# A gated delta-rule attention between two slot FFNs: the turns of the query in transpose mode, fill instructions in the first turn, and a new order of all groups

## The chip, the cores and the metric

The kernel runs on one core of a Trainium2 chip. The metric is the device time of one execution in microseconds; the time of the kernel before is the median of 3 runs. Everything is float32.

## What is computed

```python
x = L0_attn_x                                   # (2, 4096, 512)
x = x + 0.5 * ffn(layernorm(x))                 # slot FFN: route each token to 8 of 64 slots, pool, GRU, read back
x = x + attn(layernorm(x))                      # below
x = x + 0.5 * ffn(layernorm(x))
# attn, 16 heads of 32, for every token t:
#   q, k l2-normalised;  a = sigmoid(x Wa + ba);  b = sigmoid(x Wb + bb)
#   state = a * state + k (b * (v - state^T k))^T ;  y = state^T q
#   out = (rmsnorm(y, g_norm) * silu(x Wg)) @ Wo
```

The slots of an FFN depend on all tokens, so the program has three passes over the tokens: the routing of the first FFN, then one loop that does the first FFN's output, the attention and the routing of the second FFN, then the second FFN's output.

## The kernel before

The sequence is cut into 32 blocks of 128 tokens (`NT`), each for 2 batches (`b`). The middle loop has one turn for each block; in a turn stand pieces of up to four blocks, which the code calls `p` (the newest: FFN output, layer norm, projections of k, q, v), `q` (decays, gram matrices of keys and queries, and the inverse of the 32x32 coupling of each chunk), `r` (the attention itself and its output) and `s` (routing of the second FFN). A block's attention is done in 4 chunks of 32 tokens (`NC`), with 32x32 tiles of TensorE for each head.

Every engine has its order written out by hand: `step_pe`, `step_act`, `step_dve`, `step_pool` and `step_sp` list the calls of one turn, `first_...` and `last_...` those of the ends. An engine does its list strictly in order, and semaphores join the lists: `S[name]` counts what has been done for all blocks and batches, and `free(...)` in a function of TensorE waits until the PSUM bank that it writes has been read by its last user. The bank of each result is in the tables `..._at` (8 banks of 128x512).

The calls that matter here, with the line by which the profile names them:

- `proj_k`, `proj_q`, `proj_va`, `proj_vb` (L847) and `proj_g` (L891): the projections, full 128x128 weights; `first_xT`, `last_xT` (L690): turns of the normalised input, by `nc.tensor.transpose`.
- `gram` (L926), `apply_uw` (L945), `apply_gy` (L976, L983), `chain` (L996): 32x32 tiles. `apply_uw` needs the inverse, which comes through DRAM (`inverse_out`, `inverse_in`, L537).
- `qe_T` (L961): a matmul of the decayed query (`qa`) with the identity, which puts the turned query under the sums of `apply_gy`; two for a part, two parts for each batch.
- `cum` (L899, L901) and `dec` (L911): running sums of the decays; `out_proj` (L1011), `y_norm` (L1004); `hidden` (L1028), `logits` (L1040), `slots` (L1048), `alpha_T` (L1051): the second FFN's routing; `ffn` (L836): the first FFN's output.
- On ScalarE `gate_of` (L1667), `last_gelu` (L1726), `query_square` (L1648), `dec_exp` (L1684). On VectorE `last_top` (L2327 on), `last_weights` (L2336 on), `second_sum` (L2570), `invert` (L2540, L2542), `reading` (L2527), `chunk_kept` (L2553), `state` (L2559), `first_sum` (L2441), `query_turn` (L2508). On GpSimd `query_power` (L1977).

Of the kernel before, what the change touches and what calls it, by code (L numbers as in the profile page):

```python
# [27 lines left out]
P = 128  # L28
# [7 lines left out]
def build(nc, x, Wq, Wk, Wv, Wa, ba, Wb, bb, Wg, Wo, g_norm, slot_init, slot_scale, w1, b1, w2, b2,  # L36
          wih, whh, bih, bhh, wv, bv, wo, bo, tau, out):
    ctx = ExitStack()
    with ctx:
# [169 lines left out]
        ffn_at = [banks(1, 1), banks(2, 1)]  # L209
        xT_at = [banks(1, 1), banks(7, 1)]  # L210
        k_at = [banks(6, 1), banks(0, 1)]
        q_at = [banks(4, 1), banks(4, 1)]
        va_at = [banks(1, 1), banks(5, 1)]
        vb_at = [banks(5, 1), banks(4, 1)]
        g_at = [banks(0, 1), banks(7, 1)]
        dec_at = [banks(5, 1), banks(0, 1)]
        ones_at = [banks(1, 1)[:, 0:1], banks(6, 1)[:, 0:1]]
        wo_at = [banks(2, 1), banks(0, 1)]
        rxT_at = [banks(1, 1), banks(0, 1)]
        h_at = [banks(3, 1), banks(2, 1)]  # L220
        lg_at = [banks(7, 1)[:, 0:NS], banks(0, 1)[:, 0:NS]]
        y_at = [banks(6, 2), banks(5, 2)]
        cum_at = banks(6, 1)[:, 0:8 * H]
        aT_at = banks(4, 1)[:, 0:P]
        slot_at = banks(2, 1)
        gram_at = [[banks(1, 1), banks(5, 1)], [banks(4, 1), banks(3, 1)]]
        uw_at = [[banks(0, 1), banks(7, 1)], [banks(1, 1), banks(5, 1)]]
        gq_at = [[banks(3, 1), banks(2, 1)], [banks(0, 1), banks(1, 1)]]
# [172 lines left out]
        def _(sp):  # L401
# [188 lines left out]
            def last_sp():  # L590
                store_second(NT - 2, 0)
                hold(NT - 1, 0)
                store_second(NT - 2, 1)
                store_alpha(NT - 3)
# [3 lines left out]
                inverse_in(NT - 1, 1)  # L598
                coupling_out(NT, 0)
# [5 lines left out]
                store_alpha(NT - 2)  # L605
# [3 lines left out]
                inverse_in(NT, 1)  # L609
                drain_loads()  # L610
# [5 lines left out]
            def first_sp():  # L616
# [4 lines left out]
                load_first(2, 0)  # L621
                load_first(2, 1)
                coupling_out(1, 0)
                coupling_out(1, 1)
                coupling_in(1)
                hold(1, 0)
                load_alpha(3)
                load_first(3, 0)
                hold(1, 1)
                inverse_out(1)  # L630
                load_first(3, 1)
# [5 lines left out]
                store_second(1, 0)  # L637
                hold(2, 0)
                load_alpha(4)
                store_second(1, 1)  # L640
                load_first(4, 0)
                hold(2, 1)
                inverse_out(2)
                load_first(4, 1)
# [25 lines left out]
            for t in range(4, NT):  # L670
                step_sp(t + 1, t, t - 1, t - 2, t - 3)
# [13 lines left out]
        def _(pe):  # L685
# [2251 lines left out]
```

## Time and profile before

| | |
|---|---|
| time, median of 3 runs | 2709.87 us (2707.37 to 2710.03) |
| profiled execution | 2713.64 us, its span 2711.0 us |
| TensorE busy | 2597.6 us, 96% of the span |
| VectorE, GpSimd, ScalarE busy | 68%, 49%, 41% |
| granted TensorE clock, mean | 0.985 |

The span has a routing pass of some 300 us, the middle loop from 310.5 us to about 2640 us, and the last pass. Matmuls are pipelined: a row's duration reaches to the modelled end of the last one, so the pace of TensorE is read from the start of one row to the start of the next. In a timeline a row merges neighbours of one line: start, length, engine, line, operation, names, shape, and in brackets how long the engine was idle before it and who ended that. A float32 matmul stands in the trace as two passes, each with its own weight load; a transpose as one.

### The profile page before, as it was taken

How to read it: one execution, taken by the hardware profiler on the slowest of the kernel's cores; microseconds unless marked ns; L12 is line 12 of the kernel's file. 1: busy time of each engine (PE TensorE's matmuls, PEld its weight loads, DVE VectorE, ACT ScalarE, POOL GpSimd, SP SyncE). 2: the span in 40 equal slices, each digit the busy share in tenths (PEclk: the TensorE clock that was granted, in tenths of full speed). 3: DMA queues.
4: the chain of work that ended last, by engine and by line, in shares of the span. 5: the costliest groups of instructions: out<-in, count | busy, mean ns of one | idle time of the engine just before them, and what ended most of it. 6: DMA issues, size and time to landing. Idle time of an engine off the chain costs nothing.

```text
span 2711.0 us, 116416 instructions
## 1 busy us (share of the span) xinstructions
PE 2597.6 (96%) x51052; PEld 1857.1 (69%) x51052; DVE 1849.7 (68%) x5306; ACT 1122.9 (41%) x2024; POOL 1334.0 (49%) x1767
## 2 busy tenths in 40 slices
PE   7999879999999999999999999999999999999868
PEld 5788557777766677677766676777667777776643
DVE  6778456776777766676666666666666776777626
ACT  5777324343333333444334444443444334333320
POOL 2222255555555555555555555555555555555510
PEclk9999989999999999999999999999999999999979
DMA  7443022222222222222222222222222222222178
GB/s 232 113 133 115 22 57 66 67 67 67 67 67 61 60 61 63 58 67 67 67 67 67 65 64 66 55 60 62 64 67 67 67 67 67 67 67 58 52 265 326
DMA packets 365963, 224.74 MB, mean 83 GB/s; under 512 B 277584, under 2 KB 294032, under 8 KB 365456
## 3 DMA queue, kind: packets, MB, share of 16 engines
q1 hardware_dynamic: 356240, 200.51, 26.6%
q10 hardware_dynamic: 9216, 16.78, 1.6%
q8 instruction: 402, 6.59, 1.0%
q14 instruction: 105, 0.86, 0.1%
HBM read 125.49 MB, written 74.97 MB: 74 GB/s over the span
## 4 chain that ended last, share of the span: by engine, by line
PE 62%; DVE 15%; issue 10%; ACT 6%; POOL 5%; SPq 1%; DMA 1%; DVEq 0%; ACTq 0%; POOLq 0%
PE psum L847 14%; PE psum L945 5%; PE psum L1011 4%; PE psum L926 4%; PE psum L891 4%; PE psum L976 4%; PE psum L996 4%; PE psum L983 3%; DVE blk L2542 3%; DVE blk L2540 3%; PE psum L753 2%; PE psum L911 2%; PE psum L961 2%; PE psum L1028 2%; POOL sm L1977 2%
## 5 line engine op out<-in xcount | busy, mean ns | idle before, releaser
L847 PE MATMUL psum<-w_all,xnT 128*128 128x512 f32 (+2 forms) x2048 | 751.0, 501 | 6.7 <-DVE pk L2527 6.0
L1977 POOL TENSOR_TENSOR sm<-sm,half 128x1 f32<-128x1 f32 (+1 forms) x384 | 537.0, 1398 | 142.6 <-ACT sm L1672 126.6
L847 PEld LDWEIGHTS psum<-w_all,xnT 128*128 128x128 f32 x2048 | 366.4, 191 | 229.4 <-issue 178.6
L2540 DVE TENSOR_TENSOR blk<-blk 128x30 f32<-128x30 f32 (+14 forms) x960 | 328.0, 342 | 37.1 <-issue 10.6
L2542 DVE TENSOR_TENSOR blk<-blk 128x30 f32<-128x30 f32 (+14 forms) x960 | 324.0, 338 | 33.0
L2009 POOL TENSOR_SCALAR sm<-sm 128x1 f32<-128x1 f32 x64 | 22.4, 351 | 541.1 <-DVE sm L2447 541.1
L891 PEld LDWEIGHTS psum<-xnT,w_all 128*128 128x128 f32 x2048 | 246.7, 191 | 49.1 <-issue 39.9
L891 PE MATMUL psum<-xnT,w_all 128*128 128x128 f32 x2048 | 273.7, 282 | 0.0
L1011 PE MATMUL psum<-w_out,gate 128*128 128x512 f32 x512 | 260.7, 612 | 0.0
L996 PEld LDWEIGHTS psum<-qg,st 32*32 32x32 f32 x8192 | 127.4, 105 | 94.9 <-issue 55.5
L2492 DVE TENSOR_REDUCE sm<-scr 128x16 f32<-128x512 f32 x64 | 43.9, 686 | 201.4 <-ACT scr L1648 201.4
L1695 ACT ACTIVATE qg<-psum 128x256 f32<-128x256 f32 x128 | 42.1, 381 | 322.7 <-PE psum L976 322.7
L996 PE MATMUL psum<-qg,st 32*32 32x64 f32 x8192 | 167.9, 218 | 6.3 <-issue 3.8
L926 PE MATMUL psum<-kqT 32*32 32x64 f32 x8192 | 148.0, 215 | 5.5 <-DVE kqT L2508 2.1
L976 PE MATMUL psum<-pk,uw 32*32 32x64 f32 x8192 | 144.4, 224 | 7.4 <-issue 6.4
L983 PE MATMUL psum<-pk,uw 32*32 32x64 f32 x8192 | 149.6, 225 | 0.7 <-issue 0.7
L926 PEld LDWEIGHTS psum<-kqT 32*32 32x32 f32 x8192 | 124.2, 105 | 38.1 <-issue 26.7
L1028 PEld LDWEIGHTS psum<-rxT,w1T 128*128 128x128 f32 x1024 | 131.1, 194 | 19.9 <-issue 15.3
L945 PEld LDWEIGHTS psum<-vk,E 32*32 32x32 f32 x8192 | 120.8, 105 | 29.1 <-issue 25.2
L1028 PE MATMUL psum<-rxT,w1T 128*128 128x128 f32 x1024 | 140.1, 281 | 0.0
L976 PEld LDWEIGHTS psum<-pk,uw 32*32 32x32 f32 x8192 | 99.9, 103 | 54.4 <-issue 32.8
L945 PE MATMUL psum<-vk,E 32*32 32x64 f32 x8192 | 134.8, 215 | 0.0
(278 smaller groups left out, 4726.4 us busy)
## 6 DMA issues: line engine op xcount, KB each, us to landing
blk<-n_scratch SPq DMA_DIRECT2D x64, 512.0 KB, 4.2
xin<-in_L_attn_x_dram SPq DMA_DIRECT2D x96, 256.0 KB, 3.0
n_scratch<-nn SPq DMA_DIRECT2D x64, 256.0 KB, 4.1
xh<-xc SPq DMA_DIRECT2D x64, 256.0 KB, 2.2
e_scratch<-blk SPq DMA_DIRECT2D x32, 512.0 KB, 2.9
E<-e_scratch SPq DMA_DIRECT2D x64, 256.0 KB, 3.9
x_scratch<-xh SPq DMA_DIRECT2D x62, 256.0 KB, 2.5
rxn<-in_L_attn_x_dram SPq DMA_DIRECT2D x32, 256.0 KB, 3.0
```

Source lines behind the costliest of these rows:

```text
L847: last = mm(dst, xnT[b][:, k * P:(k + 1) * P], w_all[:, k * WK + at:k * WK + at + n], start=(k == 0), stop=(k == KC - 1))
L891: last = mm(g_at[b][:, part * P:(part + 1) * P], w_all[:, at:at + P], xnT[b][:, k * P:(k + 1) * P], start=(k == 0), stop=(k == KC - 1))
L926: last = mm(q32(gram_at[b][part], c, at, 2 * HD), q32(kqT[b], c, h * 2 * HD, HD), q32(kqT[b], c, h * 2 * HD, 2 * HD), start=True, stop=True)
L945: last = mm(q32(uw_at[b][part], c, at, 2 * HD), q32(E[b], c, h * HD, HD), vk3[b][CH * c:CH * (c + 1), n % 2::2 - n % 2, h, :], start=True, ...
L976: last = mm(q32(gq_at[b][hb // 2], hq, (hb % 2 * NC + c) * 2 * HD, 2 * HD), q32(uw[b], c, at + HD, HD), q32(pk[b], c, at, 2 * HD), start=F ...
L983: last = mm(q32(y_at[b], hq, (hb * NC + c) * 2 * HD, 2 * HD), q32(uw[b], c, at, HD), q32(pk[b], c, at, 2 * HD), start=(hb % 2 == 0 and r = ...
L996: last = mm(q32(y_at[b], hq, at, 2 * HD), q32(st[b], hq, x * P + hb * HD, HD), q32(qg[b], hq, at, 2 * HD), start=False, stop=True, skip_gr ...
L1011: last = mm(wo_at[b], gate[b][:, part * P:(part + 1) * P], w_out[:, part * D:(part + 1) * D], start=(part == 0), stop=(part == KC - 1))
L1028: last = mm(h_at[b][:, part * P:(part + 1) * P], w1T[:, k * HID + part * P:k * HID + (part + 1) * P], rxT[b][:, k * P:(k + 1) * P], start= ...
L1977: return g.tensor_tensor(dst, a, half[:, 0:n], ALU.pow)
L2540: own(tt(o, Y[:, 0:rows, s_:s_ + 1].to_broadcast([P, rows, cols]), N[:, s_:s_ + 1, s_ + 1:CH].to_broadcast([P, rows, cols]), ALU.mult))
L2542: ins = tt(Y[:, 0:rows, s_ + 1:CH], Y[:, 0:rows, s_ + 1:CH], o, ALU.add)
```

## The change

What it does:

- `qe_T` gets `is_transpose=True`, and waits on its own semaphore for its query.
- `fill(56, 1)`: 56 small matmuls and one turn of the identity into a free bank, between `ffn(1)` and `first_xT(1, 0)`.
- All PSUM places are dealt out anew, and with them the users that `free(...)` waits for.
- The orders of all five engines are written anew. On TensorE `cum(q)` goes ahead of `dec(q, 1)`, `logits(s, 1)` behind the first half of `out_proj(r, 0)`, `apply_gy(r, 0, 0)` beside `apply_gy(r, 0, 1)`, and `proj_vb(q, 1)`, `proj_g(q, 1, 2)`, `ffn(p)`, `alpha_T(s)` to other places. On ScalarE `gate_of(q, 1)` goes ahead of `last_gelu(r, 0)`. On the SP queue `load_first` and `load_alpha` come later.
- The loop's turn is cut elsewhere (`range(5, NT + 1)`), so more stands in `first_...`. The calls are the same ones, as often, but for `fill`.

```diff
-        g_at = [banks(0, 1), banks(7, 1)]
+        g_at = [banks(4, 1), banks(3, 1)]
-        lg_at = [banks(7, 1)[:, 0:NS], banks(0, 1)[:, 0:NS]]
+        lg_at = [banks(3, 1)[:, 0:NS], banks(7, 1)[:, 0:NS]]
-        y_at = [banks(6, 2), banks(5, 2)]
+        y_at = [banks(6, 2), banks(6, 2)]
-        gram_at = [[banks(1, 1), banks(5, 1)], [banks(4, 1), banks(3, 1)]]
+        gram_at = [[banks(0, 1), banks(3, 1)], [banks(4, 1), banks(1, 1)]]
...
             def proj_g(n, b, part):
                 if part == 0:
+                    pe.wait_ge(S["xnT"], both(n, b))
                     if b == 0:
-                        free((n - 1, (T["qg"][1], nth(n - 1, 0))), (n, (S["draw"], both(n, 1))))
+                        free((n, (T["pt"][1], nth(n, 0))))
+                    else:
+                        free((n - 1, (S["yv"], both(n - 1, 0))), (n, (T["pt"][0], nth(n, 1))))
...
             def qe_T(n, b, part):
+                pe.wait_ge(S["qe"], both(n, b))
...
                     mm(eight(gq_at[b][part])[:, k * NC:(k + 1) * NC, 0:HD], qa[b][:, hb * P:(hb + 1) * P],
-                       ident[:, :].rearrange("p (c e) -> p c e", c=NC), start=(k == 0), stop=False, skip_group_check=True)
+                       ident[:, :].rearrange("p (c e) -> p c e", c=NC), start=(k == 0), stop=False, is_transpose=True,
+                       skip_group_check=True)
...
             def logits(n, b):
                 pe.wait_ge(S["hT"], both(n + NT, b))
                 if b == 0:
-                    free((n + 1, (S["gate"], both(n + 1, 1))), (n, (S["ysq"], both(n, 0))))
+                    free((n + 1, (S["gate"], both(n + 1, 1))), (n, (S["yv"], both(n, 0))))
                 else:
-                    free((n + 2, (S["draw"], both(n + 2, 1))), (n + 1, (T["uw"][0], nth(n + 1, 0))), (n, (S["rxnT"], both(n + NT, 1))))
+                    free((n + 1, (S["ysq"], both(n + 1, 0))), (n, (S["ysq"], both(n, 1))))
...
+            def fill(n, turned):
+                for i in range(n):
+                    c = i % NC
+                    mm(q32(y_at[1], c, i // NC % 8 * 2 * HD, HD), q32(ident, c, c * HD, HD), q32(ident, c, 0, HD), start=True, stop=True)
+                for c in range(turned):
+                    tr(q32(y_at[1], c, 0, HD), q32(ident, c, c * HD, HD), q32(ident, c, c * HD, HD))
...
             def first_pe():
                 ffn(1)
+                fill(56, 1)
                 first_xT(1, 0)
...
                 chain(r, 0, 1)
                 gram(q, 0, 2)
                 chain(r, 0, 2)
+                gram(q, 0, 3)
+                cum(q)
                 dec(q, 1)
-                gram(q, 0, 3)
-                logits(s, 1)
                 chain(r, 0, 3)
...
                 apply_uw(r, 1, 0)
-                cum(q)
                 out_proj(r, 0, 0)
+                out_proj(r, 0, 1)
+                logits(s, 1)
                 apply_uw(r, 1, 1)
...
+                proj_g(q, 1, 0)
+                proj_g(q, 1, 1)
                 slots(s)
-                proj_g(q, 1, 0)
                 apply_gy(r, 1, 2)
                 apply_gy(r, 1, 3)
-                proj_g(q, 1, 1)
+                proj_vb(q, 1, 0)
+                proj_g(q, 1, 2)
                 proj_g(q, 0, 0)
-                ffn(p)
                 chain(r, 1, 0)
```

The order of TensorE from the chains of `r`, batch 0 (L996 before, L1013 after), over the grams of `q` (L926, L938) to the output projection (L1011, L1032), before:

```order
L996 MATMUL psum<-qg,st 32x64 x16
L911 MATMUL psum<-dr,after 128x512
L926 MATMUL psum<-kqT 32x64 x16
L1040 MATMUL psum<-w2T,hT 128x64 x2
L996 MATMUL psum<-qg,st 32x64 x16
L926 MATMUL psum<-kqT 32x64 x64
L945 MATMUL psum<-vk,E 32x64 x16
L899 MATMUL psum<-gt,before 128x32
L899 MATMUL psum<-gt,upto 128x32
L899 MATMUL psum<-gt,after 128x32
L901 MATMUL psum<-glx,ones 32x32 x4
L1011 MATMUL psum<-w_out,gate 128x512
```

and of the change:

```order
L1013 MATMUL psum<-qg,st 32x64 x16
L938 MATMUL psum<-kqT 32x64 x16
L909 MATMUL psum<-gt,before 128x32
L909 MATMUL psum<-gt,upto 128x32
L909 MATMUL psum<-gt,after 128x32
L911 MATMUL psum<-glx,ones 32x32 x4
L921 MATMUL psum<-dr,after 128x512
L1013 MATMUL psum<-qg,st 32x64 x16
L938 MATMUL psum<-kqT 32x64 x64
L959 MATMUL psum<-vk,E 32x64 x16
L1032 MATMUL psum<-w_out,gate 128x512 x2
L1065 MATMUL psum<-w2T,hT 128x64 x2
```

The running sums (L899, L901) move from behind the grams to ahead of them, and the logits of `s` (L1040, L1065) from ahead of them to behind them.

The order of TensorE in the second half of the turn, from the last pieces of `apply_gy` of `r`, batch 1, to the first chains, before:

```order
L976 MATMUL psum<-pk,uw 32x64 x16
L983 MATMUL psum<-pk,uw 32x64 x16
L891 MATMUL psum<-xnT,w_all 128x128 x8
L836 MATMUL psum<-sv,aT_in 128x512 x2
L996 MATMUL psum<-qg,st 32x64 x16
L891 MATMUL psum<-xnT,w_all 128x128 x8
```

and of the change:

```order
L993 MATMUL psum<-pk,uw 32x64 x16
L1000 MATMUL psum<-pk,uw 32x64 x16
L848 MATMUL psum<-w_all,xnT 128x256 x2
L902 MATMUL psum<-xnT,w_all 128x128 x8
L1013 MATMUL psum<-qg,st 32x64 x16
L902 MATMUL psum<-xnT,w_all 128x128 x4
```

The gate projection of batch 0 (the second four of the first L891 row; the second four of L902) now stands behind half of `proj_vb` and ahead of the same chain; `ffn` (L836) has left this place.

The order of ScalarE near the turn's end, before:

```order
L1672 ACTIVATE sm<-psum,eps 128x1
L1715 ACTIVATE rxn<-xh,sm 128x512
L1726 ACT_TABLE_LOAD
L1726 ACTIVATE hT<-psum,h_bias 128x128 x2
L1667 ACT_TABLE_LOAD
L1667 ACTIVATE gate<-psum 128x512
L1720 ACTIVATE rxT<-psum 128x512
```

and of the change:

```order
L1707 ACTIVATE sm<-psum,eps 128x1
L1702 ACTIVATE gate<-psum 128x512
L1761 ACT_TABLE_LOAD
L1761 ACTIVATE hT<-psum,h_bias 128x128 x2
L1750 ACTIVATE rxn<-xh,sm 128x512
L1773 ACTIVATE aT_out<-psum 128x128
L1755 ACTIVATE rxT<-psum 128x512
```

The gate of `q`, batch 1 (L1667, L1702) goes ahead of the gelu (L1726, L1761), and one table load is gone there.

## Rows read from the trace of the kernel before

**Rows 1.** The page: the span.

```profile
span 2711.0 us, 116416 instructions
```

**Rows 2.** Windows, the loop's 28 turns: busy of PE, PEld, DVE, ACT, POOL, then the clock.

```profile
461.05:2437.67 1976.62, 1962.16 (x42757) 1390.18 (x42756) 1380.71 (x3781) 798.17 (x1401) 1106.48 (x1401) 1.00 0.25 64
```

**Rows 3.** Timeline of PE at the end of one turn.

```profile
1158.39 1.02 PE L847 MATMUL psum<-w_all,xnT 128*128 128x512 f32 x2
1159.64 0.63 PE L1040 MATMUL psum<-w2T,hT 128*128 128x64 f32 x4 [0.22 <-ACT gate L1667]
1160.10 1.08 PE L847 MATMUL psum<-w_all,xnT 128*128 128x256 f32 x4
1161.02 0.61 PE L961 MATMUL psum<-ident,qa 128*128 128x128 f32 x4
1161.47 1.06 PE L1028 MATMUL psum<-rxT,w1T 128*128 128x128 f32 x8
1162.36 1.02 PE L847 MATMUL psum<-w_all,xnT 128*128 128x512 f32 x2
1163.22 1.05 PE L1028 MATMUL psum<-rxT,w1T 128*128 128x128 f32 x8
1164.11 0.60 PE L690 MATMUL psum<-ident,xn 128*128 128x128 f32 x4
1164.55 1.14 PE L847 MATMUL psum<-w_all,xnT 128*128 128x288 f32 x4
...
1166.06 1.15 PE L945 MATMUL psum<-vk,E 32*32 32x64 f32 x68
```

**Rows 4.** Timelines from the last query projection to the grams of batch 1.

```profile
1110.24 0.65 PE L996 MATMUL psum<-qg,st 32*32 32x64 f32 x32
...
1112.08 2.92 POOL L1977 TENSOR_TENSOR sm<-sm,half 128x16 f32<-128x16 f32 x1
...
1115.83 0.71 DVE L2508 STREAM_TRANSPOSE kqT<-qs 128x512 f32<-128x512 f32 x1
...
1116.69 1.99 PE L926 MATMUL psum<-kqT 32*32 32x64 f32 x128
```

**Rows 5.** Timeline of PE behind those grams.

```profile
1118.47 0.65 PE L945 MATMUL psum<-vk,E 32*32 32x64 f32 x32
1119.05 0.41 PE L899 MATMUL psum<-gt,before 128*128 128x32 f32 x2
...
1120.04 1.12 PE L1011 MATMUL psum<-w_out,gate 128*128 128x512 f32 x2
...
1131.92 2.05 PE L891 MATMUL psum<-xnT,w_all 128*128 128x128 f32 x16
```

**Rows 6.** Timeline of DVE in the same stretch.

```profile
1119.08 0.27 DVE L2327 SCALAR_TENSOR_TENSOR lgt<-psum,itau,b2s 128x64 f32<-128x64 f32 x1
...
1122.77 0.98 DVE L2336 TENSOR_TENSOR lgt<-lgt 128x64 f32<-128x64 f32 x1 [0.35 <-ACT lgt L1733]
...
1126.81 0.75 DVE L2570 SCALAR_TENSOR_TENSOR xh<-psum,sm,xh 128x512 f32<-128x512 f32 x1 [1.59 <-POOL sm L1977]
...
1132.19 0.75 DVE L2553 TENSOR_TENSOR qg<-psum,qa 128x256 f32<-128x256 f32 x2 [0.32 <-ACT qg L1695]
1132.86 0.41 DVE L2527 TENSOR_TENSOR pk<-psum,dm 128x256 f32<-128x256 f32 x1
```

**Rows 7.** The inverse's load: L537's landing times, and its issue in this turn.

```profile
DMA to landing us min/median/max: 3.1/3.9/4.8
...
1161.54 1.98 SPq L537 DMA_DIRECT2D E<-e_scratch  x2
```

**Rows 8.** The first turn: timeline of PE, and a window (PE, PEld, DVE, ACT, POOL, clock).

```profile
315.72 1.12 PE L690 MATMUL psum<-ident,xn 128*128 128x128 f32 x4 [4.09 <-ACT xn L1623]
317.53 12.05 PE L847 MATMUL psum<-w_all,xnT 128*128 128x512 f32 x28 [0.69 <-ACT xnT L1628]
...
315.30:322.00 6.70, 5.59 (x10) 2.90 (x11) 0.00 (x0) 0.97 (x2) 0.91 (x3) 0.50 0.09 32
```

More of the change, by code:

```diff
@@ L1181, in last_pe @@
                 apply_uw(NT - 1, 1, 0)
-                cum(NT)
                 out_proj(NT - 1, 0, 0)
+                out_proj(NT - 1, 0, 1)
+                logits(NT - 2, 1)
                 apply_uw(NT - 1, 1, 1)
@@ new lines, in first_pe @@
+                gram(3, 1, 3)
+                apply_uw(2, 1, 0)
+                out_proj(2, 0, 0)
+                out_proj(2, 0, 1)
+                logits(1, 1)
+                apply_uw(2, 1, 1)
+                apply_uw(2, 1, 2)
+                apply_uw(2, 1, 3)
+                qe_T(2, 1, 0)
+                out_proj(2, 0, 2)
+                out_proj(2, 0, 3)
+                y_norm(2, 0)
+                qe_T(2, 1, 1)
+                apply_gy(2, 1, 0)
+                apply_gy(2, 1, 1)
@@ new lines, in first_pe @@
+                proj_g(3, 1, 0)
+                proj_g(3, 1, 1)
+                slots(1)
+                apply_gy(2, 1, 2)
+                apply_gy(2, 1, 3)
+                proj_vb(3, 1, 0)
+                proj_g(3, 1, 2)
+                proj_g(3, 0, 0)
+                chain(2, 1, 0)
+                proj_g(3, 0, 1)
+                last_xT(2, 0)
+                chain(2, 1, 1)
+                proj_g(3, 0, 2)
+                ffn(4)
+                chain(2, 1, 2)
+                proj_vb(3, 1, 1)
@@ new lines, in first_pe @@
+                proj_g(3, 0, 3)
+                chain(2, 1, 3)
+                proj_g(3, 1, 3)
+                hidden(2, 0, 0)
+                out_proj(2, 1, 0)
+                out_proj(2, 1, 1)
+                first_xT(4, 0)
+                out_proj(2, 1, 2)
+                y_norm(2, 1)
+                proj_k(4, 0, 0)
+                out_proj(2, 1, 3)
+                proj_k(4, 0, 1)
+                proj_k(4, 0, 2)
+                alpha_T(1)
+                hidden(2, 0, 1)
+                proj_q(4, 0, 0)
@@ new lines, in first_pe @@
+                proj_k(4, 0, 3)
+                logits(2, 0)
+                proj_q(4, 0, 1)
+                proj_vb(4, 0, 0)
+                proj_q(4, 0, 2)
+                proj_vb(4, 0, 1)
+                last_xT(2, 1)
+                proj_q(4, 0, 3)
+                proj_va(4, 0, 0)
+                hidden(2, 1, 0)
+                hidden(2, 1, 1)
+                qe_T(3, 0, 0)
+                first_xT(4, 1)
+                proj_va(4, 0, 1)
+                proj_va(4, 1, 0)
+                apply_uw(3, 0, 0)
```

1004 lines of the change are left out of this document (480 added, 524 removed).

## The prediction

> **What bounds the kernel now.** I read the windows first. Over 28 turns of the middle loop [rows 2] TensorE is busy 1962.16 of 1976.62 us at a granted clock of 1.00, while VectorE has 1380.71, GpSimd 1106.48 and ScalarE 798.17. The window is that of the loop's own 28 turns (`range(4, NT)`), so a turn takes 1976.62 / 28 = 70.6 us, and TensorE sets it. Busy is not pace, though: what counts is how far one row's start lies behind the start of the row ahead. So the timeline came next. There the rows hold hidden waits as well as work: two passes of 512 columns take 1163.22 - 1162.36 = 0.86 us, but from 1158.39 to the logits at 1159.64 it is 1.25 us, and the row names ScalarE's gate as what was waited for [rows 3]. The last view is what the other engines do between two such points.
>
> It shows that a turn has two kinds of stretch. From the end of the last query projection to the grams of batch 1 it takes 1116.69 - 1110.24 = 6.45 us [rows 4], and that is no work of TensorE: ScalarE's square and VectorE's sums of the query come first, then the power on GpSimd, which takes 2.92 us and ends at 1115.00, and VectorE's turn of the query ends at 1116.54, 0.15 us ahead of the grams. Whatever TensorE does meanwhile, this latency stays. The other 70.6 - 6.45 = 64.1 us are TensorE's, and only what leaves those counts.
>
> **The change, part by part, for a turn.**
>
> Turns of the query. `qe_T` is four calls in a turn, each of two matmuls, four passes, in 1161.47 - 1161.02 = 0.45 us. The nearest operation in transpose mode, `first_xT`, does four whole 128-column turns in 1164.55 - 1164.11 = 0.44 us, one pass each [rows 3]. So a call goes from 0.45 to 0.22 us; four calls give 4 x 0.225 = 0.90 us, all in the 64.1 us. The bounds are 0 (the output is written in four pieces of 32 columns, which no row in this mode has) and 0.90; I take 0.90, since pass count is what the rows differ in. The Trainium skill, "TensorE: Matmul & The Clock Gate", in its table of terms calls transpose mode four times faster for FP32; the rows show a factor of two. By the page the gain would be about 1.35 us a turn.
>
> Running sums and logits. `cum` takes 1120.04 - 1119.05 = 0.99 us [rows 5], and it moves from the 64.1 us into the 6.45 us, where there is room: TensorE's own rows there come to about 5.9 us. The output projection behind it stands alone between tile groups, and its row is 1.12 us long where the same two passes among their like make 1.02 [rows 3, 5]; two of them stand together now, so 0.1 us goes with it. `logits(s, 1)` goes the other way: 1160.10 - 1159.64 = 0.46 us [rows 3], with the border to a tile group, 0.1, 0.56 us. Net -0.99 - 0.10 + 0.56 = -0.53 us. The one excursion from tiles to full weights that the new order saves (13 instead of 14) falls in the 6.45 us and is worth nothing.
>
> The wait for the gate. `logits(r, 0)` waited 1.25 - 0.86 = 0.39 us, because the gate of `q` stood behind the gelu and a table load on ScalarE. In the new order it stands ahead, so the wait goes: -0.39 us.
>
> What is new. `last_top(s, 1)` on VectorE started at 1119.08, 0.61 us behind the end of the grams at 1118.47 [rows 5, 6]. Its logits now come only after one tile group (1119.05 - 1118.47 = 0.58), two output projections (1.82 with borders) and themselves (0.56): 2.96 us, some 0.2 more until read, so at +3.15 us. VectorE's list stands behind it: routing weights, `second_sum(r, 0)`, the inverse, `chunk_kept`, `reading(q, 1, 0)`, the states. From 1119.08 to the end of the weights at 1126.81 - 1.59 = 1125.22 it was 6.14 us, of which 0.35 were a wait for an exponential, and that may now come in time. So `second_sum` starts at +3.15 + 5.8 to 6.1 = +9.0 to +9.3 instead of +8.34, because the 1.59 us of waiting ahead of it [rows 6] absorbs most. That moves `reading(q, 1, 0)`, which ended at 1132.86 + 0.41 = +14.8 us, to about +15.3 (0.7 to 0.95 later, less the wait of 0.32 us ahead of `chunk_kept` [rows 6], which absorbs some as well). And `proj_g(q, 0, 0)` now writes the bank that `reading(q, 1, 0)` reads. It began one call behind 1131.92, at +14.1 to +14.4 us; now it loses 0.99 of `cum`, 0.45 of two turns of the query and some 0.3 of borders, and gets 0.56, 0.86 (`proj_vb`) and 0.89 (`proj_g`) ahead of it: +14.7. It waits about 0.6 us. Behind it on TensorE stand the chains of batch 1, `ffn(p)` and `first_xT(p, 0)`. `first_sum(p, 0)` moved behind `invert(q, 13, 16)`, 2.5 us later, and the normalised input would be ready about +27.2 to +28.3; TensorE comes there at about +28.1 once it has waited the 0.6, so I charge the two once. Bounds: 0 (VectorE in time) and 2.5 us (its whole delay of 3.15 - 0.61); I take +0.6.
>
> The inverse. `apply_uw(q, 0, 0)` started at 1166.06, 4.52 us behind the issue of its load at 1161.54, which lands after 3.1 to 4.8 us, the batch-0 half first [rows 3, 7]. So it has about 1 us to spare. TensorE gets there 1.2 us sooner; VectorE's waits that TensorE caused (for the chains and for the second output projection) shrink by about as much. I take 0, bounds 0 and +0.6.
>
> Other moves: `proj_vb`, `alpha_T`, `load_first` and `load_alpha` (still 3 us and more ahead of their users), 0 each, and small waits, ±0.1.
>
> Sum for a turn: -0.90 - 0.53 - 0.39 + 0.60 = -1.2 us (-1.22).
>
> Number of turns. 28 are in the window; the first and the last ones, where TensorE waits more, count for about 2 more: 30 x 1.22 = 36.6 us.
>
> The first turn. TensorE was idle 4.09 us ahead of `first_xT(1, 0)` [rows 8]; the fill (112 short passes) fits in there. The granted clock was 0.50, the 1.2 GHz level, from 315.3 to 322.0 us, and projections started at 317.53, so 4.5 us went at half pace: keeping the clock would be worth 2.2 us, bounds 0 and 2.8. In turn two, `first_sum(2, 0)` comes 2.5 us later, which work moved ahead of it repays in part. I take -1 for both together. The ends: 0, ±4.
>
> Total -37.6 us. The profiled execution took 2713.6 us (its span 2711.0 [rows 1] and 2.6 around it), 3.8 over the median of the runs. 2713.6 - 37.6 = 2676.0, and on the scale of the median 2672.3. I say 2673.
>
> **Rivals.** About 0.2% (5.4 us) is what a measurement can tell from no change.
>
> 1. The forecast, -0.8 to -1.5 us a turn, 2664 to 2686: chance 0.50.
> 2. VectorE is in time after all (the ops of `last_weights` were slowed by GpSimd's work beside them, and it is spread otherwise now), so the 0.6 doesn't appear: -1.8 us a turn, 54 us with 30 turns, 2655. For it: the delay is a difference of sums of some 15 us each. Down to 2640 if the 6.45 us shrink too. 0.22.
> 3. The inverse binds: `apply_uw` waits for its load, and a turn can only lose the spare 1 us less what VectorE loses by the later `last_top`, 0.3 to 0.7 us: -9 to -21 us, 2689 to 2701. For it: the slack is small in each turn. Against it: VectorE's list waited for TensorE in that stretch. 0.12.
> 4. The transposes cost what the matmuls did: -0.3 us a turn, 2700. Against it: no row has such a matmul in one pass at two passes' pace. 0.05.
> 5. Slower: the late logits. If `proj_g(q, 0, 0)` and the chains behind it take VectorE's whole 2.5 us, a turn gets 2.5 - 1.82 = 0.7 us longer, 21 us in all, 2731. It decides once the wait there is over 1.8 us. Against it: the 1.59 us of waiting ahead of `second_sum`, which must stay necessary for some other reason, such as the output projection or GpSimd's power coming later. 0.07.
> 6. The clock. 17 turns by TensorE stand in each turn of the loop already, 8 more come, and the granted clock is 1.00 throughout [rows 2]. Should a stretch of 6.7 us at the lower level, as in [rows 8], come once a turn, it would cost up to 3.3 us a turn, 100 us: 2810. The Trainium skill, on the same page under "PE-mode transpose", says that this mode doesn't count as busy for the clock; by that rule this would be its way. 0.01. What is left, 0.03, is no change within 5.4 us by small waits that eat it up.
>
> The range: 8 in 10 takes rivals 1 and 2 and the nearer part of 3: 2646 to 2697. Faster by over 0.2%: 0.50 + 0.22 + 0.12 + 0.05, less what 3 and 4 have near 2704, so 0.88. Slower 0.08, the same 0.04.
>
> **What would show it.** The window of 28 turns at 69.4 us each. L976 (the new `qe_T`) 256 passes in all instead of 512, two of them in 0.22 us. No wait for the gate ahead of `logits(r, 0)`. A wait of about 0.6 us for `reading` ahead of `proj_g(q, 0, 0)`, VectorE idle some 2.4 us ahead of `last_top(s, 1)` and none ahead of `second_sum(r, 0)`. 6.4 to 6.5 us from the last query projection to the grams. The clock at 1.00 from 315 to 322 us. Wrong would be: `apply_uw` waiting for the inverse, the 6.45 us changed, or a wait of more than 1 us at a place not named.

## Result: 0.7% slower

The changed kernel takes 2730.09 us (median of 7 runs, 2722.05 to 2735.78) against 2710.03 us (median of 7, 2707.37 to 2717.83) on the same chip: ratio 1.0066, 95% interval 1.0046 to 1.0085. I had forecast 2673 us. The order did what was worked out at nearly every place, and yet a turn, measured between the same points of turns 2 and 32, went from 70.5 us to 71.2 us instead of 69.4.

The page of the changed kernel, its span, its busy times and one queue of section 3 (packets, MB, share), beside [rows 1]:

```profile
span 2731.6 us, 116548 instructions
PE 2560.2 (94%) x50909; PEld 1828.3 (67%) x50909; DVE 1841.9 (67%) x5306; ACT 1053.9 (39%) x1962; POOL 1328.8 (49%) x1767
q8 instruction: 402, 6.59, 1.0%
```

TensorE's groups by line, kernel before. The columns are busy us, mean ns, then the idle time ahead of them and what ended it; L976 and L983 are the two halves of `apply_gy`, L926 is `gram`, L945 `apply_uw`:

```profile
L983 PE MATMUL psum<-pk,uw 32*32 32x64 f32 x8192 | 149.6, 225 | 0.7 <-issue 0.7
L926 PE MATMUL psum<-kqT 32*32 32x64 f32 x8192 | 148.0, 215 | 5.5 <-DVE kqT L2508 2.1 <-ACT dr L1684 2.1
L976 PE MATMUL psum<-pk,uw 32*32 32x64 f32 x8192 | 144.4, 224 | 7.4 <-issue 6.4 <-ACT uw L1689 0.7
L945 PE MATMUL psum<-vk,E 32*32 32x64 f32 x8192 | 134.8, 215 | 0.0
```

The same view of the changed kernel (L993 and L1000 `apply_gy`, L938 `gram`, L959 `apply_uw`), with `proj_g` (L902) and the query's turns (L976):

```profile
L902 PE MATMUL psum<-xnT,w_all 128*128 128x128 f32 x2048 | 279.8, 284 | 24.7 <-DVE pk L2562 24.7
...
L938 PE MATMUL psum<-kqT 32*32 32x64 f32 x8192 | 158.9, 216 | 11.0 <-issue 7.7 <-DVE kqT L2543 1.3 <-DVE kn L2523 1.1
L1000 PE MATMUL psum<-pk,uw 32*32 32x64 f32 x8192 | 152.2, 225 | 30.1 <-issue 30.1
L993 PE MATMUL psum<-pk,uw 32*32 32x64 f32 x8192 | 150.6, 224 | 17.3 <-issue 16.5 <-ACT uw L1724 0.4
L959 PE MATMUL psum<-vk,E 32*32 32x64 f32 x8192 | 140.1, 217 | 18.5 <-issue 14.4 <-DMA E<-e_scratch 4.2
...
L976 PE MATMUL psum<-ident,qa 128*128 128x128 f32 x256 | 53.8, 292 | 0.0
```

The reader is to see the word "issue". It is idle time that no wait for an engine or a transfer explains. In these four small-tile lines it was 0.7 + 6.4 = 7.1 us in all, and is 7.7 + 30.1 + 16.5 + 14.4 = 68.7 us. The difference, 61.6 us, is about what separates forecast and result (57 us).

Where does it stand? Timeline of TensorE in the changed kernel, the two `apply_gy` that now stand side by side, first in one turn, then in the turn before it:

```profile
1179.03 0.45 PE L993 MATMUL psum<-pk,uw 32*32 32x64 f32 x32
1179.29 0.54 PE L1000 MATMUL psum<-pk,uw 32*32 32x64 f32 x29
...
1180.01 0.26 PE L1000 MATMUL psum<-pk,uw 32*32 32x64 f32 x4
1181.33 0.43 PE L1000 MATMUL psum<-pk,uw 32*32 32x64 f32 x25 [1.06 <-issue]
1181.68 0.70 PE L848 MATMUL psum<-w_all,xnT 128*128 128x512 f32 x1
```

```profile
1109.44 0.45 PE L993 MATMUL psum<-pk,uw 32*32 32x64 f32 x32
1109.70 0.54 PE L1000 MATMUL psum<-pk,uw 32*32 32x64 f32 x29
...
1110.42 0.49 PE L1000 MATMUL psum<-pk,uw 32*32 32x64 f32 x29
1110.84 1.98 PE L848 MATMUL psum<-w_all,xnT 128*128 128x512 f32 x4
```

The last L1000 row breaks in two behind its fourth pass: 1.06 us idle in the middle of a group of equal passes, of one call, with no wait in the code there. In the other turn it runs through. No semaphore stands there that could do it.

**The theory.** TensorE's instructions come in packets through queue q8, and TensorE idles where the next packet is late. I numbered all of TensorE's records (weight loads, passes, semaphore instructions) in order of time. There are 103084; divided by 256 that is 402.7, and q8 moved 402 packets, of 16384 bytes each in the trace, 64 bytes an instruction. The gaps of changing length, in both kernels, stand at records whose number leaves 192 on division by 256, to within two records. Such a place is called a border here, and the 256 records between two borders a group. There are 402 borders in either kernel, 403 in `fill120` and 400 in `b_transp` (two of the runs below), each time as many as q8 has packets; why the rest is 192 and not 0 no run tells. Of TensorE's idle stretches over 0.15 us between 320 and 2640 us, those at a border add up to 10.9 us in the kernel before and to 72.1 us in the changed one. The Trainium skill, "Advanced Engine Details and Errata", section "ISA Cache", gives an instruction cache line as 16 KB or 256 instructions; the trace agrees with that size. In both kernels a turn has exactly 3072 = 12 x 256 records, so the twelve borders stand at the same instructions in every turn. The times of q8's packets show the rest: a packet starts about 0.9 us after the border ahead of it when nothing disturbs it, takes 0.9 to 1.4 us, and no group starts sooner than about 1.2 us after its packet's end, in either kernel. So a group whose next packet starts behind its border needs about 3.2 us (an estimate from these three); full-width work takes 5 to 20 us for one, but 128 passes of 32x32 tiles, with their weight loads, take 3 to 4, and if the packet is late TensorE runs dry. With the n-th packet taken with the n-th border, in the loop of the kernel before no packet of 337 starts more than 2 us behind its border, and 82 start ahead of it; in the changed kernel 83 of 335 start more than 2 us behind.

The same records, by place in the turn: gap at the border, in ns, from the start of one pass to the start of the next, mean of 23 turns and from the least to the most, and how long behind the border the next packet starts, in us. In brackets stand the block (a dot for any), the batch and the piece.

```
changed kernel        gap (ns)           next packet     before           gap (ns)
ahead of apply_uw      112               +2.33           ffn(p)           446 (318-534)
apply_uw(q,0)          402 (35-1501)     +2.38           gram(q,1)         34
apply_gy(q,0,1)        889 (11-1545)     +2.83           gram(r+1,0)       60
gram / apply_gy(q,0,3) 367 (16-1121)     +1.43           apply_uw(1)       35
gram(.,0,3)            226 (67-630)      +1.54           apply_gy          11
gram(.,1)              101 (24-195)      +1.22           apply_gy          27
apply_gy(.,1,1)         11               +2.52           apply_gy(.,1,2)  168 (8-528)
apply_gy(.,1,2)        654 (73-1156)     +1.87           others           as without a border
```

Less what such a place takes anyway (11 to 36 ns, and 109 ahead of `apply_uw`), that is 2.49 us a turn in the changed kernel. In the kernel before it is 0.16 in `apply_gy` and 0.41 in `ffn`, which took 1.47 us on average there and takes 1.06 in every turn of the changed kernel, where no border stands in it: 0.57. The difference, 1.92 us a turn, times 30 is 57.6 us.

Four packets start 2.3 us and more behind their border. Two of them have large transfers beside them: the one ahead of `apply_uw(q,0,0)` has the two loads of E (the inverse that `apply_uw` needs, L537 before), and the one at `apply_gy(.,1,1)` the loads of the coupling that `invert` works on. The other two, in `apply_uw(q,0)` and `apply_gy(q,0,1)`, have no transfer beside them and stand right behind the first. DMA view of the changed kernel from 1030.9 to 1036.18 us (busy tenths in 40 slices):

```profile
DMA  0599999999998999999999961000001000000000
```

The border is at 1031.7, the engines are full until 1033.9, the packet starts at 1033.76, and `apply_gy(q,0,1)` then has a gap of 1.27 us. The two go together in 26 of 27 turns: in the four in which this packet starts by +0.76 us, `apply_gy(q,0,1)` has no gap, and in the 22 in which it starts at +2.04 us or later, the gap is 0.99 to 1.55 us.

### The profile page after: what moved, and what is told of

It is laid out like the page before. It is cut to its first block, busy times and chain, and to the rows that moved or that the text cites. A ratio compares the mean times of both kernels' runs of the same rounds, so it can differ in the third digit from the quotient of the medians.

```text
span 2731.6 us, 116548 instructions
## 1 busy us (share of the span) xinstructions
PE 2560.2 (94%) x50909; PEld 1828.3 (67%) x50909; DVE 1841.9 (67%) x5306; ACT 1053.9 (39%) x1962; POOL 1328.8 (49%) x1767
## 4 chain that ended last, share of the span: by engine, by line
PE 77%; DVE 9%; issue 6%; POOL 4%; ACT 1%; DMA 1%; SPq 1%; POOLq 0%; DVEq 0%; ACTq 0%
PE psum L848 25%; PE psum L902 7%; PE psum L1032 6%; PE psum L1013 5%; PE psum L1053 4%; PE psum L938 4%; PE psum L959 4%; PE psum L690 3%; PE psum L1000 3%; PE psum L993 3%; PE psum L753 2%; PE psum L921 2%; DVE blk L2577 2%; DVE blk L2575 2%; PE psum L835 1%
## 5 line engine op out<-in xcount | busy, mean ns | idle before, releaser
L2575 DVE TENSOR_TENSOR blk<-blk 128x30 f32<-128x30 f32 (+14 forms) x960 | 332.4, 346 | 61.0 <-issue 34.5
L2577 DVE TENSOR_TENSOR blk<-blk 128x30 f32<-128x30 f32 (+14 forms) x960 | 334.7, 349 | 33.0
L902 PE MATMUL psum<-xnT,w_all 128*128 128x128 f32 x2048 | 279.8, 284 | 24.7 <-DVE pk L2562 24.7
L902 PEld LDWEIGHTS psum<-xnT,w_all 128*128 128x128 f32 x2048 | 253.0, 193 | 42.7 <-issue 27.7
L2044 POOL TENSOR_SCALAR sm<-sm 128x1 f32<-128x1 f32 x64 | 14.9, 233 | 495.1 <-DVE sm L2482 495.1
L1032 PE MATMUL psum<-w_out,gate 128*128 128x512 f32 x512 | 250.6, 603 | 0.0
L1013 PEld LDWEIGHTS psum<-qg,st 32*32 32x32 f32 x8192 | 126.3, 105 | 117.3 <-issue 61.3
L1000 PE MATMUL psum<-pk,uw 32*32 32x64 f32 x8192 | 152.2, 225 | 30.1 <-issue 30.1
L1013 PE MATMUL psum<-qg,st 32*32 32x64 f32 x8192 | 168.0, 218 | 6.7 <-issue 2.6
L938 PE MATMUL psum<-kqT 32*32 32x64 f32 x8192 | 158.9, 216 | 11.0 <-issue 7.7
L993 PE MATMUL psum<-pk,uw 32*32 32x64 f32 x8192 | 150.6, 224 | 17.3 <-issue 16.5
L1724 ACT ACTIVATE uw<-psum 128x512 f32<-128x512 f32 x128 | 76.5, 597 | 220.8 <-PE psum L959 220.8
L938 PEld LDWEIGHTS psum<-kqT 32*32 32x32 f32 x8192 | 130.4, 105 | 46.1 <-issue 38.4
L959 PE MATMUL psum<-vk,E 32*32 32x64 f32 x8192 | 140.1, 217 | 18.5 <-issue 14.4
L993 PEld LDWEIGHTS psum<-pk,uw 32*32 32x32 f32 x8192 | 104.8, 103 | 76.3 <-issue 75.5
L959 PEld LDWEIGHTS psum<-vk,E 32*32 32x32 f32 x8192 | 123.9, 106 | 34.6 <-issue 27.7
L1053 PE MATMUL psum<-rxT,w1T 128*128 128x128 f32 x1024 | 133.9, 280 | 2.4 <-ACT rxT L1755 1.6
L1000 PEld LDWEIGHTS psum<-pk,uw 32*32 32x32 f32 x8192 | 112.2, 103 | 33.7 <-issue 33.7
```

The lines of the kernel that those rows point to most:

```text
L902: last = mm(g_at[b][:, part * P:(part + 1) * P], w_all[:, at:at + P], xnT[b][:, k * P:(k + 1) * P], start=(k == 0), stop=(k == KC - 1))
L938: last = mm(q32(gram_at[b][part], c, at, 2 * HD), q32(kqT[b], c, h * 2 * HD, HD), q32(kqT[b], c, h * 2 * HD, 2 * HD), start=True, stop=True)
L959: last = mm(q32(uw_at[b][part], c, at, 2 * HD), q32(E[b], c, h * HD, HD), vk3[b][CH * c:CH * (c + 1), n % 2::2 - n % 2, h, :], start=True, ...
L993: last = mm(q32(gq_at[b][hb // 2], hq, (hb % 2 * NC + c) * 2 * HD, 2 * HD), q32(uw[b], c, at + HD, HD), q32(pk[b], c, at, 2 * HD), start=F ...
L1000: last = mm(q32(y_at[b], hq, (hb * NC + c) * 2 * HD, 2 * HD), q32(uw[b], c, at, HD), q32(pk[b], c, at, 2 * HD), start=(hb % 2 == 0 and r = ...
L1013: last = mm(q32(y_at[b], hq, at, 2 * HD), q32(st[b], hq, x * P + hb * HD, HD), q32(qg[b], hq, at, 2 * HD), start=False, stop=True, skip_gr ...
```

## Experiments

Eleven kernels ran. The rivals were the semaphore waits (the late logits and `proj_g`'s wait for VectorE, rival 5 of the prediction), the fill instructions themselves, and the two `apply_gy` side by side. The clock is looked at with `before_128`.

**Moving the borders and nothing else.** A fill matmul has four records, so 64 more move every border by a whole packet, and 32 fewer by half of one.

```diff
-                fill(56, 1)
+                fill(120, 1)        # fill120;  fill24: fill(24, 1)
```

> The changed kernel with 120 fill instructions in the first turn in place of 56. Every later instruction of TensorE's stream moves on by 256 records (64 more fill instructions of 4 records each), one whole 16384-byte packet of the instruction queue, so the borders between packets stand at the same instructions as in the changed kernel. Border theory (TensorE waits where one packet's 256 instructions are run through faster than the next packet comes): a turn stays 71.1 us, the time 2728 to 2734 us with at most 3 us for the longer fill. Rival (waits for semaphores, set by VectorE and late logits, make the loss): the same. A control for the next run: if this one moves by more than 5 us, the fill itself matters and not the borders.

> The changed kernel with 24 fill instructions in place of 56: nothing else differs, but every packet border of TensorE's instruction stream stands 128 instructions later in the turn. Border theory: the waits in the middle of L1000, L993 and L959 vanish from their places and others stand 128 instructions away; worked out from the gaps of one turn, two packets of the 12 would then last only 1.4 to 1.8 us, so I expect the time to move by more than 10 us, and rather up, to 2740 to 2800 us; a fall below 2720 would also be of this theory. Rival (semaphore waits make the loss): the turns' order and every wait for another engine are unchanged, so 2730 within 4 us.

`fill120`: 2727.14 us, ratio to before 1.0061 (1.0046 to 1.0076). It is as fast as the changed kernel, and its page counts one packet more:

```profile
q8 instruction: 403, 6.60, 1.0%
```

`fill24`: 2846.83 us, ratio 1.0497 (1.0480 to 1.0515), 117 us slower than the changed kernel with 32 fill instructions fewer, and above the 2740 to 2800 that I expected. Its groups by line:

```profile
L902 PE MATMUL psum<-xnT,w_all 128*128 128x128 f32 x2048 | 296.5, 298 | 11.1 <-DVE pk L2562 11.1
L1000 PE MATMUL psum<-pk,uw 32*32 32x64 f32 x8192 | 158.7, 226 | 105.4 <-issue 105.4
L959 PE MATMUL psum<-vk,E 32*32 32x64 f32 x8192 | 153.4, 218 | 52.7 <-issue 46.6 <-DMA E<-e_scratch 4.3
L938 PE MATMUL psum<-kqT 32*32 32x64 f32 x8192 | 147.3, 216 | 4.1 <-issue 1.7 <-DVE kqT L2543 1.3 <-DVE kn L2523 1.1
```

The gaps changed places: L938 has 1.7 us of issue now and had 7.7, L1000 has 105.4. The wait for VectorE in `proj_g` fell from 24.7 to 11.1 us while the kernel got slower (in the loop alone from 13.7 to nothing; the rest stands in the first turn). So that wait isn't what makes the time, and neither is the length of the fill.

**One part of the change, in the kernel before.** The query's turns in transpose mode alone; then the same with 16 records a turn of waits for a value long reached, so that the turn has 3072 records and the borders stand as before.

```diff
-   ident[:, :]..., start=(k == 0), stop=False, skip_group_check=True)
+   ident[:, :]..., start=(k == 0), stop=False, is_transpose=True, skip_group_check=True)
+   # b_transp_pad, ahead of each of these matmuls:
+   for _ in range(3 if b + part + k else 12):
+       pe.wait_ge(S["qe"], both(n, b))
```

> The kernel before with one edit: the query turns in transpose mode (half the passes). By the prediction's own term (0.90 us a turn, 30 turns) it takes 2683 us, if nothing behind it has to wait. Its turn has 3056 TensorE records in place of 3072, so the packet borders walk by 16 instructions from turn to turn. Border theory: turns of unequal length (more than 1 us between the shortest and the longest as the borders pass dense tile groups), and part of the 27 us is lost: 2685 to 2710 us. Rival (borders don't matter): turns equal within 0.3 us, 2683 us within 4. Rival (transpose mode saves nothing): 2710.

> As the run before, with 16 further records a turn in TensorE's stream, waits on semaphores that have long been reached, so that the turn has 3072 records again and each packet border stands where it stands in the kernel before. Border theory: the turns are equal again but for the waits at two borders that the kernel before has too; 2680 to 2695 us, at or under the run before. Rival (borders don't matter, the 16 waits cost up to 0.05 us each): 2683 to 2700, at or above the run before.

`b_transp`: 2812.49 us, ratio 1.0372 (1.0357 to 1.0387). The kernel has less work and takes 102 us more than the kernel before beside it. That is in the direction of the theory, but far beyond the 2685 to 2710 that I expected of it. Turns 5 to 15 take 72.9 to 77.0 us, turns 16 to 19, where the borders have walked back to their good places, 70.5, 69.8, 71.6 and 71.6, and the turns behind them up to 76.5. `b_transp_pad`: 2694.26 us, ratio 0.9937 (0.9922 to 0.9952), most turns 69.7 to 70.1 us. So 16 instructions a turn that do nothing are worth 118 us. Groups of the run without and of the run with them:

```profile
L983 PE MATMUL psum<-pk,uw 32*32 32x64 f32 x8192 | 156.2, 225 | 27.9 <-issue 27.8
L926 PE MATMUL psum<-kqT 32*32 32x64 f32 x8192 | 153.4, 216 | 31.9 <-issue 26.5 <-DVE kqT L2508 2.1 <-ACT dr L1684 2.1
L945 PE MATMUL psum<-vk,E 32*32 32x64 f32 x8192 | 150.6, 225 | 11.9 <-issue 11.6
L976 PE MATMUL psum<-pk,uw 32*32 32x64 f32 x8192 | 143.6, 223 | 24.1 <-issue 23.1 <-ACT uw L1689 0.7
```

```profile
L985 PE MATMUL psum<-pk,uw 32*32 32x64 f32 x8192 | 149.3, 226 | 1.2 <-issue 1.2
L926 PE MATMUL psum<-kqT 32*32 32x64 f32 x8192 | 148.0, 216 | 5.4 <-DVE kqT L2512 2.1 <-ACT dr L1688 2.1
L978 PE MATMUL psum<-pk,uw 32*32 32x64 f32 x8192 | 143.4, 224 | 6.9 <-issue 5.8 <-ACT uw L1693 0.7
L945 PE MATMUL psum<-vk,E 32*32 32x64 f32 x8192 | 135.9, 216 | 5.0 <-issue 4.1 <-DMA E<-e_scratch 0.7
```

**Is the kernel before as sensitive?** 128 records more ahead of its first turn, nothing else.

```diff
             def first_pe():
+                for _ in range(256):
+                    pe.wait_ge(at_in, 16)
                 ffn(1)
```

> The kernel before with 128 records more ahead of its first turn (256 waits on a semaphore that has long been reached, two to a record) and nothing else: its turns keep their 3072 records, and every border between instruction packets stands 128 records earlier in the turn. Border theory: the kernel before is no less sensitive than the changed one, it only stands at a favourable phase, as its twelve borders have one gap over 0.2 us; in the other phase groups of 1.9, 1.5 and 2.9 us follow groups of normal length, so 2760 to 2860 us. Rival (only the changed order is sensitive): 2712 to 2722 us, at most 7 us for the waits themselves.

2898.69 us, ratio 1.0708 (1.0692 to 1.0725): 190 us by the place of the borders alone, more than I expected. Its turns wait in `apply_uw` and `apply_gy`. Both lines, then one such gap, between the grams and the first `apply_uw` of batch 1, and the window 1 us behind it, whose clock is third from the end:

```profile
L945 PE MATMUL psum<-vk,E 32*32 32x64 f32 x8192 | 156.8, 234 | 54.4 <-issue 54.3
L976 PE MATMUL psum<-pk,uw 32*32 32x64 f32 x8192 | 154.8, 223 | 68.3 <-issue 67.1 <-ACT uw L1691 0.7
```

```profile
1337.44 0.65 PE L945 MATMUL psum<-vk,E 32*32 32x64 f32 x32 [1.50 <-issue]
...
1338.50:1341.90 3.40, 3.40 (x38) 1.77 (x41) 0.78 (x5) 0.28 (x1) 2.03 (x3) 0.50 0.55 83
```

The gaps cost more than their own length. In the small-tile lines "issue" grew from 7.1 to 122.2 us, which explains 115 of the 190. But the granted clock also fell to 0.50, the 1.2 GHz level, 29 times between 470 and 2700 us, each time right behind such a gap, of 1.4 to 2.05 us; in the kernel before it doesn't fall there from 470 to 2550 us. About half of these gaps have such a fall behind them. The stretches at that level add up to 219 us against 84 (mean granted clock 0.963 against 0.985), so up to 67 us, an estimate by half of the difference, went with the clock. The two together come to 182. In `fill24` these stretches add up to 175 us against 93 in the changed kernel, up to 41 us, and in `b_transp` to 145 against 84, up to 30 us. The changed kernel itself has hardly more of them than the kernel before.

**The transfers in a packet's way.** The second load of E is read some 25 us later than the first, so it can wait; TensorE's stream stays as it is. In the trace it is issued 14 to 16 us behind the border ahead of `apply_uw`, where it was issued 1.3 us ahead of it. Beside it two small shifts of the borders (60 and 64 fill instructions).

```diff
                 inverse_in(r, 0)
-                inverse_in(r, 1)
                 store_alpha(u)
+                sp.wait_ge(y1_turn[0], NC * r)
+                inverse_in(r, 1)
```

> The changed kernel with the second of the two 256-KB loads of E issued some 15 us later, once apply_gy of the first batch is done (it is read some 25 us later); TensorE's stream is unchanged. In the changed kernel the two loads keep the DMA engines full from 0.4 us ahead of the packet border in front of apply_uw(q,0,0) to 2.3 us behind it; in 18 of 22 turns the next instruction packet starts only as they end, and then apply_uw and the two adjacent apply_gy behind it run into gaps of up to 1.5 us. Collision theory: with one load the packet starts about 1 us after the border, the mean gap in L1000 falls from 0.94 us to under 0.3, that in L959 from 0.38 to under 0.1; 1 to 1.7 us a turn, 2680 to 2700 us. Rival (the two apply_gy side by side starve the stream whatever the transfers do): the gaps in L1000 stay, 2725 to 2735 us. Rival (semaphore waits): 2730.

> The changed kernel with 60 fill instructions in place of 56, which puts every border 16 records earlier in the turn. Border theory: a small shift, most groups keep their length within 0.1 us, except that the group ahead of the chain turns grows from 4.1 to 4.6 us and the one behind it from 5.1 to 6.7 while the one at apply_uw falls to 3.6 us; the border ahead of apply_uw comes 0.7 us earlier against the loads of E. I expect 2715 to 2740 us, no more than 15 us from 2728 in either direction.

> The changed kernel with 64 fill instructions: every border 32 records earlier. The border ahead of apply_uw then comes 1.6 us earlier, so that its packet is fetched ahead of the loads of E (gap in apply_gy small), but the group ahead of the chain turns lasts only 2.9 us in place of 4.1, for a new gap of 0.3 to 1.3 us there. Border theory: 2710 to 2745 us. Rival (no borders): 2728 within 3.

`e1_later`: 2709.22 us, ratio 0.9975 (0.9958 to 0.9991). That is 18 to 21 us better than the changed kernel and its repeat, which ran on another chip, and some 24 us by the ratios; I had expected 30 to 50, and the time is outside my 2680 to 2700. The mean gap in `apply_gy(q,0,1)` fell from 0.89 to 0.38 us and the one behind it from 0.37 to 0.04, and the packet fetched in `apply_uw` starts at +1.69 in place of +2.38 us; but the one ahead of `apply_uw` still starts at +2.05 and the gap in `apply_uw` stays (0.42 us). These means hide two kinds of turns: in 19 of 28 the packet ahead of `apply_uw` now starts by +1.9 us and `apply_gy(q,0,1)` has no gap, in the other nine it starts at +3.2 us or later and the gap is 0.98 to 1.55 us. So the transfers are a cause: with one of the two moved, nine turns have the gap that 22 had, and the two `apply_gy` side by side don't make it alone. That the first load, which can't move, makes the rest is argued; no run moved it. The line, 30.1 us in the changed kernel:

```profile
L1001 PE MATMUL psum<-pk,uw 32*32 32x64 f32 x8192 | 149.0, 225 | 14.5 <-issue 14.5
```

`fill60`: 2716.07 us, ratio 0.9999 (0.9979 to 1.0018); `fill64`: 2715.21 us, ratio 1.0001 (0.9979 to 1.0024). Both are as fast as the kernel before and within what was expected. With 60 the gaps in `gram` are gone: the packet behind the border in the chains now starts 0.4 us ahead of that border on average, where it started 1.0 us behind. With 64 the one in `apply_uw` falls to 0.17 us, and one of 0.72 us grows ahead of `proj_g`.

**Together.** Both edits; then also a wait that was to hold back the store of x and the next load of x past a border; then 62 fill instructions.

```diff
                 coupling_in(q)
+                sp.wait_ge(y1_turn[1], NC * (r - 1) + 2)     # fill60_e1_x and fill62_e1_x
                 store_second(r, 0)
```

> Both edits that helped: 60 fill instructions and the second load of E issued once apply_gy of the first batch is done. If borders and colliding transfers are the cause, the gaps left at the border in apply_uw and the two apply_gy behind it (0.40, 0.54 and 0.19 us a turn with 60 fill instructions alone) mostly go: 0.6 to 0.9 us a turn, 2690 to 2703 us. Rival (the two edits help by the same gap and don't add): 2706 to 2716 us, as either alone.

> As the run before, and the store of x and the load of the next x, which run into the border in the second adjacent apply_gy pair (its packet comes 2.6 us late and the next border, in L993, has a gap of 0.69 us), are held back until apply_gy(r,1,1) is done, about 3 us. Collision theory: the gap in L993 falls from 0.69 to under 0.3 us, 2675 to 2695 us. Rival (the loads of the coupling, 512 KB issued 4 us ahead of that border, are what delays the packet): the gap stays, 2690 to 2703. Rival (the next x comes too late for ScalarE): a wait of first_xT for ScalarE appears and the time is above the run before.

> As the fastest run so far (2686.7 us) with 62 fill instructions in place of 60: every border 8 records earlier again. Border theory: between the gaps at 60 and at 64 fill instructions, where the border ahead of proj_g grows from 0.14 to 0.72 us and the one in apply_uw falls from 0.40 to 0.17: 2680 to 2700 us. No rival tells another number; the run looks for the phase's optimum.

`fill60_e1`: 2689.51 us, ratio 0.9921 (0.9905 to 0.9936). The two edits nearly add: against the changed kernel's 1.0066 they give 0.0067 and 0.0091 alone and 0.0145 together. `fill60_e1_x`: 2686.67 us, ratio 0.9899 (0.9883 to 0.9916). `fill62_e1_x`: 2686.62 us, ratio 0.9928 (0.9901 to 0.9956). The three can't be told apart. The wait held x back by nothing: the store of x (L585) was issued 3.52 us behind the first load of the coupling (L523) without it and 3.56 us with it. SP queue of `fill60_e1`, then of `fill60_e1_x`:

```profile
1050.59 0.33 SPq L523 DMA_DIRECT2D blk<-n_scratch  x1
1054.11 0.32 SPq L585 DMA_DIRECT2D x_scratch<-xh  x1
...
1048.51 0.33 SPq L523 DMA_DIRECT2D blk<-n_scratch  x1
1052.07 0.32 SPq L585 DMA_DIRECT2D x_scratch<-xh  x1
```

So the gap in `apply_gy(.,1,2)`, which stayed at 0.61 us, says nothing on x. Whether x or the coupling's 512 KB, issued 1.9 us ahead of the border, delays its packet was not tried. `fill60_e1_x` is 1.0% faster than the kernel before and, by the ratios, 1.7% faster than the changed one. Its lines:

```profile
L995 PE MATMUL psum<-pk,uw 32*32 32x64 f32 x8192 | 152.3, 224 | 26.3 <-issue 26.0
...
L961 PE MATMUL psum<-vk,E 32*32 32x64 f32 x8192 | 138.1, 217 | 12.1 <-issue 8.1
L1002 PE MATMUL psum<-pk,uw 32*32 32x64 f32 x8192 | 148.4, 224 | 1.0 <-issue 1.0
```

## Why the prediction was wrong

The step that failed is the first: "Whatever TensorE does meanwhile, this latency stays. The other 70.6 - 6.45 = 64.1 us are TensorE's, and only what leaves those counts." The sum then priced every call by the rows of its kind, as if a call cost the same wherever it stands. It doesn't: the order decides which calls share a packet of 256 instructions, and what transfers run as the next is fetched. That term, +1.92 us a turn, was missing: -1.22 + 1.92 = +0.70 us against +0.67 measured, and -37.6 + 57.6 = +20.0 us against the +20.1 between the medians. That the last two agree to 0.1 us is luck: the sum has 1 us for the first turn, where half of that came (below), and the 1.92 is a mean of 23 turns.

Point by point:

- **Turns of the query, -0.90: right.** 256 passes, two in 0.22 us. The factor of two stands, not the four of the Trainium skill's page "TensorE: Matmul & The Clock Gate", table of terms. Alone, with the borders kept (`b_transp_pad`), the four calls also took 0.90 us less, but the kernel got only 16.6 us faster and not 27, about 0.5 us a turn: 0.2 us went to a new wait of `slots` for `second_sum` and 0.2 us to a gap at the border in `apply_uw`.
- **Running sums and logits, -0.53:** not measured alone. What is left of a turn's change without the borders, 0.67 - 1.92 = -1.25 us, fits the sum of all terms, -1.22.
- **Gate wait, -0.39: right.** No row of `logits` waits for the gate any more; 31 did, for 10.1 us.
- **The latency stretch of 6.45 us: right but for a border.** It takes 6.46 us at the least and 6.62 on average, up to 7.03; before it was 6.44 to 6.45. The border in `gram(., 0, 3)` stands in it.
- **Late logits, +0.60: right.** VectorE was idle 2.33 us ahead of `last_top(s, 1)` (2.4 forecast), and `proj_g(q, 0, 0)` waited for `reading` in 17 of the loop's turns, 0.7 to 1.06 us each; averaged over all turns it began 0.57 us later than the call usually does. Of the 24.7 us in L902's row, 10.1 are one wait in the first turn. Only that no wait would be left ahead of `second_sum(r, 0)` was wrong, 0.58 us remained. Rival 5 gives nearly the measured time, 2731, by a mechanism that isn't there: it needed a wait over 1.8 us, and none in the loop is over 1.06. The sign that did come is the last one the prediction names, a wait of more than 1 us at a place not named.

Timeline of VectorE and of TensorE, changed kernel:

```profile
1131.33 0.28 DVE L2362 SCALAR_TENSOR_TENSOR lgt<-psum,itau,b2s 128x64 f32<-128x64 f32 x1 [2.33 <-PE psum L1065]
...
1136.26 0.75 DVE L2605 SCALAR_TENSOR_TENSOR xh<-psum,sm,xh 128x512 f32<-128x512 f32 x1 [0.58 <-POOL sm L2012]
```

```profile
1143.86 0.68 PE L902 MATMUL psum<-xnT,w_all 128*128 128x128 f32 x4 [0.82 <-DVE pk L2562]
```

- **The inverse, 0: right.** No turn of the loop waits for it. The 4.2 us in L959's row are one wait, at the last block, at 2596.8 us.
- **The first turn, -1: over-sized.** The fill didn't keep the clock: windows of the changed kernel (PE, PEld, DVE, ACT, POOL, clock) show 0.50, the 1.2 GHz level, until 319.7. From `first_xT` to the first gram it takes 20.3 us against 20.6, so 0.3 us was gained. `first_xT` itself began 1.8 us sooner, which no term had; by `apply_uw` of the second block 0.5 us was left of all this.

```profile
315.70:317.70 2.00, 2.00 (x3) 0.97 (x4) 0.00 (x0) 0.00 (x0) 0.00 (x0) 0.50 0.00 0
317.70:319.70 2.00, 2.00 (x4) 0.88 (x3) 0.00 (x0) 0.00 (x0) 0.00 (x0) 0.50 0.00 0
319.70:321.70 2.00, 2.00 (x6) 0.79 (x5) 0.00 (x0) 0.00 (x0) 0.00 (x0) 0.99 0.00 0
```

Each term of a turn that was measured was thus near its size, and the mechanism behind the result was in none of them, nor in a rival. A trace of it was there to read: 6.4 us "<-issue" in L976 of the kernel before, which the prediction passes over.

## What stays open

With the loads of E in flight, the packet ahead of `apply_uw` got through early (+0.56 to +0.76 us) in four turns and started about at their end or later in the others; what decides it no run tells. Nor why in `apply_uw(q,0)` and `apply_gy(q,0,1)` packets without any transfer beside them start 2 us and more behind their borders once the one ahead was late, nor what lets 82 packets of the kernel before start ahead of theirs. Which transfer delays the packet ahead of `apply_gy(.,1,2)` is open too.

## What to carry to other kernels

Where TensorE runs many small tiles, count its instructions: 256 to a packet, weight loads, passes and semaphore instructions alike, and see which packets are run through in under 4 us. Idle time "<-issue" in the middle of equal passes that comes and goes between turns is the sign. Look at the granted clock with it: in `before_128` about half of the gaps of 1.4 to 2.05 us had a stretch at 1.2 GHz behind them. Whoever removes an instruction from a loop shifts all those borders, so pad the loop to a whole number of packets, try some phases, and keep large transfers off the borders ahead of small-tile work, before judging the order itself.

## What the runs showed of the hardware

- The same program, with 128 instructions that do nothing ahead of its loop, took 2899 in place of 2708 us.
- Gaps at the border in `apply_gy(q,0,1)` came in steps: 11, 993 to 999, 1267 to 1272 and 1542 to 1545 ns, some 275 ns apart.
- A group run through in 1.4 us left no gap behind it where 7.2 us of slower work stood ahead: its next packet had started 2.1 us ahead of the border (kernel before). Behind normal groups a group of 1.5 us left 1.8 us (`fill24`).
- All 29 falls of the granted clock to 0.50 in the loop of `before_128` came right behind a gap of 1.4 to 2.05 us in TensorE's stream; the kernel before, without such gaps, has none in its loop.
